# Expert choice in two halves of the tokens, shifts in alternate halves of a bank, an unrolled prologue, and the residual moved behind the token groups

## The reference

```python
xn = _layernorm(x)
# attention: 8 heads, query and key of 2 channels per head, value of 16
scores = einsum('bmhd,bnhd->bhmn', q, k) / sqrt(2)
scores = where(scores >= 0, scores, 0.2 * scores)
att = gamma * (softmax(scores) @ v) + xn
# experts: 16, the best two for each token, a capacity of 1024 rows each
probs = softmax(rmsnorm(xn) @ router_weight.T + router_bias)
gate_vals, expert_idx = top_k(probs, 2)
# expert 0 gives zero, 1 a copy, 2 and 3 constants, 4 to 15 an MLP 128 -> 512 -> 128 with GELU
# tokens over the capacity are dropped; the two gates are normed to sum 1
out = x + att + combined / gate_sums
```

## Time and profile before

| | us |
|---|---|
| median of 3 runs (1012.07 to 1012.57) | 1012.35 |
| the profiled execution | 1010.73 |
| its span | 1008.9 |
| PE busy | 895.7 (89%) |
| DVE busy | 757.3 (75%) |
| ACT busy | 711.5 (71%) |
| POOL busy | 557.1 (55%) |

### The profile page before, as it was taken

One profiled execution on the slowest core, in us unless ns is written; L12 is line 12 of the kernel. 1 busy time (PEld: TensorE's weight loads), 2 busy tenths in 40 slices (PEclk: granted clock), 3 DMA queues, 4 the chain that ended last, 5 costly groups with the idle time before them and its releaser, 6 DMA issues.

```text
span 1008.9 us, 20380 instructions
## 1 busy us (share of the span) xinstructions
PE 895.7 (89%) x7619; PEld 373.0 (37%) x7620; DVE 757.3 (75%) x900; ACT 711.5 (71%) x859; POOL 557.1 (55%) x574
## 2 busy tenths in 40 slices
PE   0665642999999999999999989999999999999997
PEld 0433320233333333477777752333332333333332
DVE  6566769999999999300000039999999999999996
ACT  0786741888888888644454448888888888888886
POOL 2232331777567665499997003756657476564671
PEclk9986775999999999999999989999999999999999
DMA  8622110010110101132432310001102002002100
GB/s 246 226 46 48 36 36 26 24 45 31 35 39 23 30 23 55 45 107 89 130 111 85 131 56 15 27 18 47 33 12 57 21 22 65 17 18 61 29 7 22
DMA packets 48161, 55.32 MB, mean 55 GB/s; under 512 B 10714, under 2 KB 35122, under 8 KB 48080
## 3 DMA queue, kind: packets, MB, share of 16 engines
q1 hardware_dynamic: 38464, 44.10, 14.4%
q0 software_dynamic: 8192, 9.37, 3.2%
q10 hardware_dynamic: 1424, 0.76, 0.3%
HBM read 31.58 MB, written 30.02 MB: 61 GB/s over the span
## 4 chain that ended last, share of the span: by engine, by line
PE 76%; ACT 11%; issue 5%; DVE 5%; SPq 1%; DMA 1%; ACTq 1%; DVEq 0%; POOL 0%; POOLq 0%
PE ps L762 25%; PE ps L742 14%; PE ps L732 13%; PE ps L822 8%; PE ps L814 8%; ACT pr L634 4%; PE ps L772 3%; ACT ot L626 2%; ACT y L606 1%; PE ps L692 1%; SPq L256 1%; PE ps L803 1%; ACT pr L585 1%; PE ps L696 1%; DMA y<-in_x 1%
## 5 line engine op out<-in xcount | busy, mean ns | idle before, releaser
L1037 DVE TENSOR_SCALAR ps<-ps 128x1024 f32<-128x1024 f32 x512 | 610.4, 1228 | 20.2 <-PE ps L732 6.1
L634 ACT ACTIVATE pr<-ps 128x1024 f32<-128x1024 f32 x512 | 523.3, 1024 | 122.0 <-PE ps L742 111.8
L762 PE MATMUL ps<-pr,vp 128*32 128x256 f32 x4096 | 327.0, 392 | 0.3
L742 PE MATMUL ps<-q,kz 64*128 64x512 bf16 x1024 | 201.3, 390 | 8.6 <-DVE ps L1037 8.4
L732 PE MATMUL ps<-q,kz 62*128 62x512 bf16 x1024 | 199.4, 386 | 7.9 <-DMA q<-parts_dram 1.5
L451 POOL DMA_INDIRECT xs<-eout,idxs x128 | 129.0, 1008 | 108.5 <-ACT pr L634 78.2
L436 POOL DMA_INDIRECT disp<-xs,idxs x128 | 125.5, 980 | 45.9 <-issue 29.5
L1049 DVE TENSOR_TENSOR pr<-ps,parts 128x1024 f32<-128x1024 f32 x12 | 14.7, 1225 | 165.7 <-PE ps L822 165.7
L742 PEld LDWEIGHTS ps<-q,kz 64*128 64x128 bf16 x1024 | 49.1, 93 | 221.5 <-DVE ps L1037 114.6
L762 PEld LDWEIGHTS ps<-pr,vp 128*32 128x32 f32 x4096 | 81.1, 108 | 107.2 <-issue 90.3
L661 ACT ACTIVATE pr<-ps,b1s 128x512 f32<-128x512 f32 x96 | 66.0, 687 | 51.0 <-PE ps L814 50.8
(11 more groups left out here) (120 smaller groups left out, 601.9 us busy)
## 6 DMA issues: line engine op xcount, KB each, us to landing
disp<-pr SPq DMA_DIRECT2D x12, 512.0 KB, 4.9
eout<-pr SPq DMA_DIRECT2D x12, 512.0 KB, 2.9
y<-in_x SPq DMA_DIRECT2D x8, 512.0 KB, 7.9
out<-y SPq DMA_DIRECT2D x8, 512.0 KB, 3.3
w<-in_w1t SPq DMA_DIRECT2D x12, 256.0 KB, 3.1
w<-in_w2t SPq DMA_DIRECT2D x12, 256.0 KB, 3.3
xs<-disp SPq DMA_DIRECT2D x6, 512.0 KB, 4.8
pr<-disp SPq DMA_DIRECT2D x6, 512.0 KB, 4.7
```

The source lines that it names most:

```text
L634: act.activation(pr[:, c % BUFS, 2 * pair:2 * pair + 2, :], ring[i % RING], ACT.Exp, scale=SLOPE).then_inc(S["exps"], 1)
L742: last = pe.matmul(ring[i % RING][:, k, :], kz[r:r + TILE, hg, pair, kc * P:(kc + 1) * P], q2[r:r + TILE, hg, qh * HALF:(qh + 1) * HALF], ...
L762: last = pe.matmul(acc[p % 2][32 * g:32 * g + 32, cols], vp[:, hg, kc, g, :], pr[:, c % BUFS, g % PAIRS * 2 + g // PAIRS, cols], start=(kc ...
L1037: dve.tensor_scalar(s, s, 0.0, 1.0 / SLOPE - 1.0, ALU.max, ALU.mult).then_inc(S["relu"], 1)
```

## The change

- **No loops in the prologue.** `groups` writes out all 22 steps, with fixed offsets, on all five engines.
- **Shifts in alternate bank halves.** Even sequences use rows 0 to 63 of `ps_u`, `ub` and `shift`, odd ones rows 64 to 127. PE and ACT wait for the shift of the sequence before the last, not of the last.
- **Expert choice in two halves.** `first_choice`, `second_value` and `second_choice` take a half k of the tokens. The first half (sequences 0 to 3, groups 0 to 7) goes behind the steps 9, 11 and 12 on DVE, between `xn` of that step and `xs` of the next; the second half behind steps 16, 18 and 19, where the whole stood.
- **Residual during routing.** ACT makes the residual behind all its group steps, 64 activations, with the expert exponential behind the sixth of eight sequences. POOL waits for all of it (`y_upd`) before it copies the first values and before its routing arithmetic.
- The memset of the first gates moves ahead of the groups.

```diff
-            for n in range(LAGS):
-                step(locate(n // 2, n % 2))
-            with engine.Fori(LAGS // 2, B) as b:
-                for u in range(2):
-                    step(locate(b, u))
-            for n in range(LAGS):
-                step(locate(B + n // 2, n % 2))
+            for n in range(2 * B + LAGS):
+                step(locate(n))
                 if n in meanwhile:
                     meanwhile[n]()
+
+        def shift_rows(b):
+
+            return slice(2 * HP * (b % 2), 2 * HP * (b % 2) + 2 * HP)
...
-            pool.wait_ge(S["y_upd"], 2 * B)
+            pool.wait_ge(S["y_upd"], B)
...
-                        wait_done(act, "shift_rdy", b)
-                        act.copy(ub[:], ps_u).then_inc(S["ub_rdy"], 1)
+                        wait_done(act, "shift_rdy", b - 1)
+                        act.copy(ub[shift_rows(b), :], ps_u[shift_rows(b), :]).then_inc(S["ub_rdy"], 1)
...
-                    for t in range(GT):
-                        tt = bass.ds(b * TB + u * GT + t, 1)
-                        yt = y[:, tt, :].rearrange("p a c -> p (a c)")
-                        last = act.activation(yt, yt, ACT.Identity, scale=y_scale[:, tt], bias=y_bias[:, tt])
-                    last.then_inc(S["y_upd"], 1)
...
-                act.wait_ge(S["off_rdy"], 1)
+                act.wait_ge(S["off_rdy"], 2)
                 act.activation(gate[:, 1, :], inv, ACT.Exp).then_inc(S["r_exp"], 1)
...
-            groups(act, prologue)
-            expert_exponentials()
+            def residual(b):
+
+                for t in range(b * TB, (b + 1) * TB):
+                    last = act.activation(y[:, t, :], y[:, t, :], ACT.Identity, scale=y_scale[:, t:t + 1],
+                                          bias=y_bias[:, t:t + 1])
+                last.then_inc(S["y_upd"], 1)
+
+            groups(prologue)
+            for b in range(B):
+                residual(b)
+                if b == B - 3:
+                    expert_exponentials()
...
-                    wait_done(pe, "shift_rdy", b)
-                    pe.matmul(ps_u[HP * u:HP * u + HP, :], bok[:], hat[:, u, :], start=True, stop=True,
-                              tile_position=(0, HP * u)).then_inc(S["u_rdy"], 1)
+                    wait_done(pe, "shift_rdy", b - 1)
+                    r = 2 * HP * (b % 2) + HP * u
+                    pe.matmul(ps_u[r:r + HP, :], bok[:], hat[:, u, :], start=True, stop=True,
+                              tile_position=(0, r)).then_inc(S["u_rdy"], 1)
...
-            groups(dve, prologue, {0: first_choice, 2: second_value, 3: second_choice})
+            dve.memset(gate[:, 0, :], 1.0)
+            groups(prologue, {B + 1: lambda: first_choice(0), B + 3: lambda: second_value(0),
+                              B + 4: lambda: second_choice(0), 2 * B: lambda: first_choice(1),
+                              2 * B + 2: lambda: second_value(1), 2 * B + 3: lambda: second_choice(1)})
```

More of the change, by code:

```diff
@@ L142, in build @@
         bok = sb("bok", [P, HP], BF16)
-        ub = sb("ub", [2 * HP, GW])
-        shift = sb("shift", [2 * HP, GW], BF16)
+        ub = sb("ub", [P, GW])
+        shift = sb("shift", [P, GW], BF16)
         kz = sb("kz", [P, NHG, PAIRS, M], BF16)
@@ L213, in wait_done, with groups, locate @@
                 engine.wait_ge(S[name], count)
-        def groups(engine, step, meanwhile={}):
-            def locate(b, u):
+        def groups(step, meanwhile={}):
+            def locate(n):
                 def at(lag):
[L224 to L227, removed]
-                return at
-            for n in range(LAGS):
-                step(locate(n // 2, n % 2))
-            with engine.Fori(LAGS // 2, B) as b:
-                for u in range(2):
-                    step(locate(b, u))
-            for n in range(LAGS):
-                step(locate(B + n // 2, n % 2))
+                    m = n - lag
+                    return (m // 2, m % 2, m) if 0 <= m < 2 * B else None
+                return at
+            for n in range(2 * B + LAGS):
+                step(locate(n))
                 if n in meanwhile:
                     meanwhile[n]()
+        def shift_rows(b):
+            return slice(2 * HP * (b % 2), 2 * HP * (b % 2) + 2 * HP)
         ONE = 1
@@ L287, in store_parts @@
                             sp.dma_start(parts_dram[0, NPROD * H:NROW * H, bass.ds(b * M + v * GW, GW)],
-                                         shift[HP * v:HP * v + H, :]).then_inc(S[f"shift_out{v}"], 16)
-            groups(sp, store_parts)
+                                         shift[2 * HP * (b % 2) + HP * v:2 * HP * (b % 2) + HP * v + H, :]).then_inc(S[f"shift_out{v}"], 16)
+            groups(store_parts)
             for u in range(2):
@@ L714, in prologue @@
                     last.then_inc(S["dir_rdy"], 1)
-            groups(pe, prologue)
+            groups(prologue)
             for n, (lhs, rhs) in enumerate(((cbf[:, C_TRI:C_TRI + P], cnt), (onesb[:], incl))):
@@ L905, in prologue @@
                             wait_done(dve, f"shift_out{v}", 16 * b)
-                        dve.scalar_tensor_tensor(out=shift[:], in0=ps_u, scalar=1.0 / SLOPE, in1=ub[:],
+                        rows = shift_rows(b)
+                        dve.scalar_tensor_tensor(out=shift[rows, :], in0=ps_u[rows, :], scalar=1.0 / SLOPE, in1=ub[rows, :],
                                                  op0=ALU.mult, op1=ALU.max).then_inc(S["shift_rdy"], 1)
@@ L964, in first_choice @@
-            def first_choice():
-                dve.wait_ge(S["zero_in"], 16 * E_MLP)
[L967 to L978, removed]
@@ L980, in second_choice, with half_of, rows, per_tile @@
-            def second_choice():
-                first_of_equals(1, tiles_of(ex), second)
-            groups(dve, prologue, {0: first_choice, 2: second_value, 3: second_choice})
+            NH = NT // 2
+            descb = cbf[:, C_DESC:C_DESC + E].unsqueeze(1).broadcast_to([P, NH, E])
+            def half_of(k):
+                return slice(k * NH, (k + 1) * NH)
+            def rows(v, k):
+                return tiles_of(v)[:, half_of(k), :]
+            def per_tile(v, k):
+                return v[:, half_of(k)].unsqueeze(2).broadcast_to([P, NH, E])
@@ new lines, in first_of_equals @@
+            def first_of_equals(c, k, value, largest):
+                ranks = rows(rank_of, k)
+                link(dve.tensor_tensor(ranks, value, per_tile(largest, k), ALU.is_equal))
+                link(dve.tensor_tensor(ranks, ranks, descb, ALU.mult))
+                link(dve.tensor_reduce(rank[:, c, half_of(k)], ranks, AX.X, ALU.max))
+                link(dve.tensor_copy(rank_b[:, c, half_of(k)], rank[:, c, half_of(k)]))
+                link(dve.tensor_tensor(rows(onehot[c], k), ranks, per_tile(rank_b[:, c, :], k), ALU.is_equal))
@@ new lines, in first_choice, with second_value @@
+            def first_choice(k):
+                logits = lg[:, half_of(k), :]
+                dve.wait_ge(S["zero_in"], 16 * E_MLP)
+                dve.wait_ge(S["lg_rdy"], B * (k + 1))
+                link(dve.tensor_tensor(logits, logits, rb[:].unsqueeze(1).broadcast_to([P, NH, E]), ALU.add))
+                link(dve.tensor_reduce(top[:, half_of(k)], logits, AX.X, ALU.max))
+                first_of_equals(0, k, logits, top)
+            def second_value(k):
+                link(dve.scalar_tensor_tensor(out=rows(ex, k), in0=rows(oh1, k), scalar=-BELOW,
+                                              in1=lg[:, half_of(k), :], op0=ALU.mult, op1=ALU.add))
+                link(dve.tensor_reduce(second[:, half_of(k)], rows(ex, k), AX.X, ALU.max))
+                dve.tensor_tensor(inv[:, half_of(k)], second[:, half_of(k)], top[:, half_of(k)], ALU.subtract
+                                  ).then_inc(S["off_rdy"], 1)
@@ L985, in _, with second_choice @@
+            def second_choice(k):
+                first_of_equals(1, k, rows(ex, k), second)
+            dve.memset(gate[:, 0, :], 1.0)
+            groups(prologue, {B + 1: lambda: first_choice(0), B + 3: lambda: second_value(0),
+                              B + 4: lambda: second_choice(0), 2 * B: lambda: first_choice(1),
+                              2 * B + 2: lambda: second_value(1), 2 * B + 3: lambda: second_choice(1)})
             dve.tensor_tensor(cnt.rearrange("p (e t) -> p e t", t=NT), oh1.rearrange("p (t e) -> p e t", e=E),
@@ L986, in _ @@
                               oh2.rearrange("p (t e) -> p e t", e=E), ALU.add).then_inc(S["cnt_rdy"], 1)
-            dve.memset(gate[:, 0, :], 1.0)
             dve.wait_ge(S["cnt_rdy"], 1)
```

13 lines of the change are left out of this document (2 added, 11 removed).

## The result

The change takes 1001.0 us (median of 4 runs, 1000.2 to 1003.12), the kernel before 1012.21 (4 runs); the ratio is 0.9893, 95% interval 0.9876 to 0.991. It is faster by 11.2 us, clear of the noise, where 23.9 were forecast, and the time lies 1 us outside the range.

A forecast was written before the change was run, and what follows sets the result against it. Bounds named: ACT in static steps; in the loop, PE's wait for DVE's shift adds cost. Last lg at 48.6 + 51.6 + 8.7 + 1.9 = 110.8, plus 47.8 tail, gives 158.6, 23.9 us less: 988.5 us, range 982 to 1000.

The forecast's parts named there:

- Term 1: Token groups in the prologue: period falls to 4.3 us a group, putting the fourth lg at 48.6 us.
- the ring: Dependency cycle through PE, ACT and DVE in the groups: 8.6 us for two groups, 4.3 a group, taken as the period.
- Term 2: First half of the choice on DVE behind groups 9 to 12: costs 8.7 us plus one 1.9 us slow-clock spell on PE.
- Term 3: Tail after the last group's lg: residual ends 38.0 us later, seventh exponential 47.8 us later; the tail loses 3.9 us.
- the mark: Start of ACT's seventh exponential, with which the kernel's end moves: forecast at 158.6 us instead of 182.46.
- Sum: Whole kernel: lg of group 15 at 110.8 plus 47.8 gives 158.6, 23.9 us less, median 988.5 us.
- Rival 1: PE's clock keeps falling in the groups, one 1.9 us spell per two groups, 5.25 us a group: 1000 us; chance 0.16.
- Rival 2: Only DVE binds the groups, 4.0 us each, and no slow-clock spell follows the routing: 982 us; chance 0.09.
- lower bound of term 1: Shortest period allowed for a token group, DVE working back to back: 4.0 us.
- Rival 3: PE at half clock bounds the groups at 7.0 us each, so the change is slower: 1021 us; chance 0.05.
- Rival 4: A new PE wait for DVE's hat and bok replaces the shift wait, 6.2 to 6.5 us a group: 1012 us; chance 0.02.
- The rule weighed: Skill's clock rule for PE in the groups: matmuls that wait in every iteration are throttled anew and pay warm-up each time.

The follow-up runs named there:

- r1: Kernel before with only the prologue written out, no other part of the change, on a slower chip: 1120.9 us, ratio 0.9972.
- r2: Kernel before with the prologue written out and shifts in alternate bank halves, on a slower chip: 1107.4 us, ratio 0.986.
- r10: The change without its early half: whole expert choice at the end, residual still behind the groups: 990.2 us, ratio 0.9794.
- r11: The change with whole choice at the end, two of four residual activations in the step, the other 32 behind the groups: 984.8 us, ratio 0.9725.
- r9: Same kernel as r2 (kernel before, prologue written out, alternate halves), run on another chip: 992.9 us, ratio 0.9805.
- r12: The change with POOL's two subtractions per group on 32 of 512 columns: 988.6 us, ratio 0.9769.

## Why the prediction was wrong

- **What bounds.** Right that the loop's cost was the wait for the shift, by r1 and r2. The register work, which the change takes away as well, was worth 3 us (r1).
- **Term 1, the period: the step that failed.** I took DVE's pieces at 1.05 and 1.03 us from a stretch in which DVE had idle time, and said the DVE bound is 4.1 and the ring's 4.3. In a full DVE one of them stretches to 2.0 beside POOL in each group, and the period is 5.0: the term lacked 0.9 us of waiting for POOL, which it put at nothing without a reason. That is 2.4 us at the fourth lg (51.01 against 48.6) and 12 x 0.71 = 8.5 behind it. The prediction names POOL nowhere in this term. Rows in the trace of before had it: in the loop xs took 1.95 to 2.13 us in nine groups, with a subtraction of POOL over it. DVE, then POOL, of the kernel before:

```profile
73.07 2.05 DVE L897 TENSOR_SCALAR xs<-y,st 128x128 f32 x4 [0.17 <-DVE xn L941]
```

```profile
73.89 1.15 POOL L382 TENSOR_TENSOR parts<-ot,parts 112x512 bf16<-112x512 f32 x1 [2.50 <-ACT parts L611]
```

  They are no sign of the register work alone: POOL's instruction lies over them and ends with them. Still that work bore on what POOL's fell on, since in r1, without it, no piece is stretched. With POOL narrowed the period is 4.24, near the ring's 4.3.
- **Term 2, the early half.** 10.6 us forecast (8.7 on DVE and one spell of 1.9), 14.3 measured: 9.7 on DVE, of which 1 us because one of its products met POOL (1.37 instead of 0.42 us), and 4.6 left over. That these are PE's standing still and running at 1.2 GHz is by subtraction, not measured apart. There is not one spell but several: the mean granted clock is 0.71 to 0.78 from 76 to 126 us. By the prediction's own numbers the early half cost 10.6 us and gave back 3 at most, so its sum said that the change is better without it; it did not draw that. r10 is 11.5 us faster.
- **Term 3, the tail.** 38.0 us to the end of the residual and 47.8 to the mark, measured 38.2 and 47.8. That the residual and not the routing ends last was right. Overlooked was that DVE waits for the small exponential behind 48 of the 64 activations: the gate weights came 34 us after lg, not 28.1, and stayed hidden by only 4 us. r11 shows that half of the residual behind the groups costs nothing.
- **Sum.** 10.9 us of term 1 and 3.7 of term 2 are the 14.7 us by which lg 15 and the mark are late (125.47 against 110.8, 173.30 against 158.6), up to rounding. The median came out only 12.5 above the forecast, because the two profiled executions were not alike: that of the change lies 2.1 us above its median and that of before 1.6 below, while behind the mark the change lost 1.6 us more.
- **Rival 1** has about the number, 1000, but by luck: not the way to it. At full clock the period was 5.0 already; the spells came on top, and only behind the early half. Its sign, a granted clock under 0.8 from 40 to 100 us, did not show (0.91). Rival 2 took DVE as the bound, as it is, but at the wrong length. Its 4.0 a group, like the lower bound of term 1, is also below the 4.1 that the prediction adds up for DVE. Rival 3 did not happen: between the slow spells PE's projections at 93.2 and 114.7 us run at full clock. Rival 4 neither: no wait of PE for the shift is left.
- **The rule weighed.** PE stood idle for 4.87 us and then ran its projection in 2.04 us, three of the five projections behind it were slow too, and none of those from 40 to 80 us was. The Trainium skill's rule on the clock ("TensorE: Matmul & The Clock Gate", section "HAM oscillation — how this bites in real kernels") held for the stretch with the early half, and not for the groups before it, at 1.00.
- **The rule not weighed.** The Trainium skill ("SBUF — State Buffer", section "Who interferes with whom") says that DVE shares a pair of SBUF ports with GpSimd, that a DVE instruction with two SBUF inputs contends with a GpSimd one that reads SBUF, and one in a two-port fast mode with any, and that the first to issue keeps the ports for its whole instruction while the other is blocked. The trace agrees: xn and kmax have two SBUF operands, and where they are held they end 0.01 to 0.15 us behind POOL's instruction. xs reads one tensor from SBUF and writes SBUF, the form for which the page allows such a fast mode; it is held too, but in which mode it ran no trace shows. The reductions, lg, and hat and shift, which read one of theirs from PSUM, are never longer beside POOL. It goes both ways: POOL's subtraction at 93.50 us, where DVE was in an xn and then in an instruction of the choice, took 1.86 us instead of 1.15.

## What to carry to other kernels

A duration read in a stretch where the engine has idle time is a lower bound for the stretch in which it has none: look for the same line where it is slowest, and at what its neighbour does then. Work moved off the bounding engine of a pipeline gains little if it is put where it stands alone (r10 against r9: 2.7 us, intervals overlapping), and more if it is put where that engine waits anyway: with the whole choice at the end, half of the residual in the step and half in the tail (984.8 us) beat all in the step (992.9) and all in the tail (990.2). And a large change with a small gain is worth taking apart: here two parts gained 19 us, and two that are harmless one by one gave 8 to 10 back together.

## What the runs showed of the hardware

- DVE instructions of 0.15 to 0.34 us took up to 1.25 us beside a POOL subtraction (the longest of the 64 instructions xs and of the 64 xn in the change took 1.246 and 1.247 us, the median ones 0.335 and 0.344), and never over 0.36 us with POOL narrowed to 32 columns (r12). POOL's subtraction takes 1.15 us by itself and, in the change, up to 1.86 where DVE is in such an instruction.
- PE's granted clock differs between two runs of the same prologue: 0.94 and 0.83 over the same 60 us in r2 and r9, with lg 15 at 116.3 and 122.0. They ran on two chips, so how much of the 5.7 us is the clock is open. Within one kernel it goes with the spread of the times: the four executions of r10 had spans of 987.4, 987.8, 989.0 and 992.0 us at mean clocks of 0.973, 0.973, 0.968 and 0.967.
